# Smaller banks for transposed scores, one more for the rest: PSUM split anew in an attention and expert kernel

## What is computed

```python
sup = relu(sup_feat @ W_fc.T + b_fc)              # 8 x 1601 x 256
ref = relu(layernorm(x) @ W_fc.T + b_fc)          # 8 x 256 x 256
q, k = ref @ W_q.T + b_q, sup @ W_k.T + b_k       # in 16 heads of 16
p = softmax(einsum('bqhd,bkhd->bhqk', q, k) / 4)
out_h = einsum('bhqk,bkf->bhqf', p, sup)
attn = einsum('bhqf,hjf->bqhj', out_h, Wv) + b_v
x = x + ref + attn
x = x + experts(layernorm(x)) + shared(layernorm(x))
```

## Time and profile before

| | |
|---|---|
| median of three runs | 1262.87 us |
| span of the profiled execution | 1261.2 us |
| TensorE busy | 1210.1 us (96%) |
| TensorE weight loads | 910.0 us (72%) |
| VectorE busy | 800.7 us (63%) |
| ScalarE busy | 689.0 us (55%) |
| GpSimd busy | 361.0 us (29%) |
| exponentials (L607), 416 | 412.9 us |
| maxima of side scores (L781), 1024 | 535.2 us |

### The profile page before, as it was taken

One profiled execution on the slowest core, in us unless ns is written; L12 is line 12 of the kernel. 1 busy time (PEld: TensorE's weight loads), 2 busy tenths in 40 slices (PEclk: granted clock), 3 DMA queues, 4 the chain that ended last, 5 costly groups with the idle time before them and its releaser, 6 DMA issues. The chain is left out here.

```text
span 1261.2 us, 23345 instructions
## 1 busy us (share of the span) xinstructions
PE 1210.1 (96%) x8574; PEld 910.0 (72%) x8574; DVE 800.7 (63%) x1682; ACT 689.0 (55%) x954; POOL 361.0 (29%) x282
## 2 busy tenths in 40 slices
PE   7789999999999999999999999999999997999997
PEld 6667777777777777777777777766556885788885
DVE  4566676777777776767777676777855442444443
ACT  4446666666666666666666666656674222222221
POOL 2103233322332232323232233311202651233332
PEclk8999999999999999999999999999999998999999
DMA  5686566678768666677776666666344939733332
GB/s 146 198 229 182 171 184 172 187 208 217 211 200 236 200 191 205 193 209 217 204 220 188 195 185 172 173 187 154 87 132 174 361 129 352 217 55 51 56 53 37
DMA packets 162284, 224.94 MB, mean 178 GB/s; under 512 B 65583, under 2 KB 132023, under 8 KB 162174
## 3 DMA queue, kind: packets, MB, share of 16 engines
q1 hardware_dynamic: 147998, 191.12, 53.2%
q0 software_dynamic: 9216, 16.46, 6.1%
q10 hardware_dynamic: 4960, 15.86, 3.6%
HBM read 128.40 MB, written 93.58 MB: 176 GB/s over the span
## 5 line engine op out<-in xcount | busy, mean ns | idle before, releaser
L781 DVE TENSOR_REDUCE mx<-side 128x1 f32<-128x400 f32 (+2 forms) x1024 | 535.2, 569 | 145.6 <-PE side L505 133.9
L607 ACT ACTIVATE prob<-st 128x1024 f32<-128x1024 f32 (+1 forms) x416 | 412.9, 1022 | 180.2 <-PE st L526 178.4
L505 PE MATMUL side<-kst,qst 96*128 96x400 f32 (+2 forms) x1024 | 325.8, 377 | 4.0 <-DVE mx L781 2.6
L505 PEld LDWEIGHTS side<-kst,qst 96*128 96x128 f32 x1024 | 186.9, 188 | 114.0 <-issue 42.0
L526 PE MATMUL st<-qst,kst 97*128 97x512 f32 (+1 forms) x832 | 264.7, 400 | 1.1 <-ACT prob L607 0.4
L538 PE MATMUL acc<-prob,v 128*32 128x256 f32 (+1 forms) x3328 | 208.1, 383 | 0.0
L526 PEld LDWEIGHTS st<-qst,kst 97*128 97x128 f32 (+1 forms) x832 | 148.1, 186 | 10.4 <-ACT prob L607 2.3
L814 POOL TENSOR_TENSOR clo<-raw,chi 128x768 fp32r<-128x768 f32 (+1 forms) x32 | 60.8, 1902 | 319.5 <-ACT chi L643 319.5
L538 PEld LDWEIGHTS acc<-prob,v 128*32 128x32 f32 (+1 forms) x3328 | 94.2, 109 | 80.2 <-issue 23.6
L1715 POOL DMA_INDIRECT out<-yg,rows_of x39 | 60.8, 1558 | 163.3 <-DMA out<-yg,rows_of 104.3
L820 POOL TENSOR_TENSOR flo<-fc,fhi 128x768 fp32r<-128x768 f32 (+1 forms) x26 | 49.9, 1918 | 180.1 <-ACT fhi L659 180.1
(11 more groups left out here) (197 smaller groups left out, 1687.5 us busy)
## 6 DMA issues: line engine op xcount, KB each, us to landing
kst<-parts_at SPq DMA_DIRECT2D x90, 400.2 KB, 5.8
parts_at<-parts SPq DMA_DIRECT2D x48, 384.0 KB, 6.6
wall<-w_at ACTq DMA_DIRECT2D x10, 1536.0 KB
w_at<-piece_hi SPq DMA_DIRECT2D x27, 512.0 KB, 6.7
w_at<-piece SPq DMA_DIRECT2D x27, 512.0 KB, 5.9
v<-v_at SPq DMA_DIRECT2D x32, 408.0 KB
raw<-ctx_t SPq DMA_DIRECT2D x24, 384.0 KB, 5.5
piece<-gate_up SPq DMA_DIRECT2D x18, 512.0 KB, 4.7
```

The lines of the kernel that those rows point to most:

```text
L505: pe.matmul(side[u.bank][:, 0:w], t.qst[0:96, pair, col * P:(col + 1) * P], t.kst[0:96, pair, o:o + w], start=True, stop=True).then_inc(si ...
L607: act.activation(prob[0:rows, s, :], st[(KT * g + s) % 2][0:rows, :], ACT.Exp, scale=float(DH) ** -0.5).then_inc(exp_done, 1)
L781: dve.tensor_reduce(mx[:, p % 2, hq, r:r + 1], side[u.bank][:, 0:ranges_of(p)[r][1]], AX.X, ALU.max)\
```

## The change

The eight banks are shared out as 4 + 3 + 1. `BANKS` is 4, so a unit waits for the unit four ahead of it. The transposed scores get three tiles `st` of one bank (`SCORE_BANKS`), one for each pair of heads in turn, over all phases (`pair_tile`). Each of the two matmuls of a tile waits for the exponential three pairs earlier and tells ScalarE by itself. The exponential of a key tile goes in two, 128x512 each, and each waits for its own matmul. The product with the values waits for the second of them as before. The functions that counted units in a loop over batches go, since every unit's number is known.

```diff
-BANKS = 3
+BANKS = 4
+SCORE_BANKS = 3
...
+def pair_tile(p, s, i):
+
+    return GP * (KT * p + s) + i
...
-        st = [ctx.enter_context(nc.psum_tensor(f"st{i}", [P, 4 * NQ], F32)) for i in range(2)]
+        st = [ctx.enter_context(nc.psum_tensor(f"st{i}", [P, 2 * NQ], F32)) for i in range(SCORE_BANKS)]
...
-            after(pe, exp_done, KT * p + s - 1)
-            rows, into = key_rows(s), st[(KT * g + s) % 2]
+            rows = key_rows(s)
             for i in range(GP):
-                mm = pe.matmul(into[0:rows, i * 2 * NQ:(i + 1) * 2 * NQ],
-                               t.kst[0:97, GP * g + i, s * P:s * P + rows],
-                               t.qst[0:97, GP * g + i, :], start=True, stop=True)
-            mm.then_inc(st_full, 1)
+                n = pair_tile(p, s, i)
+                after(pe, exp_done, n - SCORE_BANKS + 1)
+                pe.matmul(st[n % SCORE_BANKS][0:rows, :], t.kst[0:97, GP * g + i, s * P:s * P + rows],
+                          t.qst[0:97, GP * g + i, :], start=True, stop=True).then_inc(st_full, 1)
 
         def pe_values(pe, p, b, g, kt):
             rows = key_rows(kt)
-            pe.wait_ge(exp_done, KT * p + kt + 1)
+            pe.wait_ge(exp_done, pair_tile(p, kt, GP - 1) + 1)
...
         def act_exp(act, p, g, s):
             rows = key_rows(s)
-            act.wait_ge(st_full, KT * p + s + 1)
             after(act, pv_done, KT * (p - 1) + s + 1)
...
-            act.activation(prob[0:rows, s, :], st[(KT * g + s) % 2][0:rows, :], ACT.Exp,
-                           scale=float(DH) ** -0.5).then_inc(exp_done, 1)
+            for i in range(GP):
+                n = pair_tile(p, s, i)
+                act.wait_ge(st_full, n + 1)
+                act.activation(prob[0:rows, s, i * 2 * NQ:(i + 1) * 2 * NQ], st[n % SCORE_BANKS][0:rows, :], ACT.Exp,
+                               scale=float(DH) ** -0.5).then_inc(exp_done, 1)
```

More of the change, by code:

```diff
@@ L218, with __init__ @@
 class Unit:
[L222 to L226, removed]
+    def __init__(self, n):
+        self.n, self.bank, self.used = n, n % BANKS, n // BANKS
     def full(self):
-        return self.count(self.n + 1, UNITS)
+        return self.n + 1
     def out(self):
-        return self.count(self.n // BANKS + 1, UNITS // BANKS)
+        return self.used + 1
     def free(self):
-        return self.count(self.n // BANKS, UNITS // BANKS)
+        return self.used
 PRE_AT = {u: n for n, u in enumerate([u for u in PRE if u[0] not in NO_BANK])}
@@ L247 @@
                     AT_END += 1
[L248 to L251, removed]
 def before_unit(u):
@@ L258, in body_unit @@
 def body_unit(b, at, g, kind, arg):
-    n = BODY_AT[at, g, kind, arg]
-    return Unit(n) if isinstance(b, int) else Unit(n, b - at)
+    return Unit(BODY_AT[at, g, kind, arg])
 def ranges_of(p):
@@ L901, in sp_lent_free @@
             unit_full(sp, body_unit(b, b, g, "S1", SCORES - 1))
-            sp.wait_ge(exp_done, KT * (LENT_FROM - 1) + 8)
+            sp.wait_ge(exp_done, pair_tile(LENT_FROM - 1, 8, 0))
             sp.wait_ge(mx_done, LENT_FROM + 1)
@@ L1017, in resid_unit @@
                 return before_unit(("xres", 0, 0))
-            return body_unit(b - 1, at - 1, 1, "xres", 0) if isinstance(b, int) else                 Unit(BODY_AT[1, 1, "xres", 0] - UNITS, b - 1)
+            return body_unit(b - 1, at - 1, 1, "xres", 0)
         def last_scores(units):
```

## The result

The changed kernel takes 1252.59 us (median of six runs, 1249.26 to 1256.68) where the kernel before took 1263.76 us beside it: a ratio of 0.9908, 95% interval 0.989 to 0.9926. That is 11.2 us faster; 1247 us, 15.5 us faster, was forecast. The profiled execution spans 1252.1 us.

A forecast was written before the change was run, and what follows sets the result against it. TensorE, held by late weight loads waiting for banks, was taken to bound the kernel. Side banks -34, start -6.5 and transposed scores +25 gave -15.5 us: from 1262.9 to 1247 us, range 1229 to 1268.

The forecast's parts named there:

- What bounds the kernel: Attention, 180 to 840 us: TensorE sets the pace, and loads waiting for banks lose 27 us in 660.
- Side banks, -34 us in the phases: Side scores and projections: a fourth bank removes the waits for banks, 1.1 us a phase over 31 phases; bounds -17 and -45.
- Ring of three, +25 us: Transposed scores at four short steps wait for the tile before's exponential, 0.8 us a phase over 31 phases; bounds +12 and +40.
- late by x costs x less 0.08: Weight loads on TensorE: a load late by x costs x less some 0.08 us.
- Exponentials: ScalarE: 832 halves at 0.60 us, 0.50 apart in a run, 33 us more ScalarE work; by itself nothing.
- The start, -6.5 us: Before 82 us: at most 3.5 us won before the keys' limit, 2.7 us free behind it; bounds -3 and -12.
- The last phase: Transposed scores of the last phase: counted within the +25 us, at 0.8 us a phase.
- small handshake: Rival: of the transposed scores' short steps only tile 2 to 3 costs, +12; 1228 us; chance 0.18.
- Given back: Rival: half of the side banks' gain returns as VectorE's backlog; 1264 us, no change; chance 0.15.
- Slower: Rival: exponential halves don't overlap, 0.65 us start to start, +26; 1273 us; chance 0.16 shared with the other slower rival.
- The banks give nothing: Rival: the named bank waits are for something else, only added cost remains; 1288 us; chance 0.16 shared with the other slower rival.
- one sign of being wrong: 180 to 840 us: waits for prob over 1.2 us a phase would show the forecast wrong.

The follow-up runs named there:

- The square: Four kernels on one chip: side banks 3 or 4 by single banks 3 or 4, without the nine-bank corner; 1262.56 (kernel before), 1261.46, 1279.77 and 1251.67 us.
- e2: Kernel before with halved exponentials, three side banks, three single banks for the transposed scores, eighth bank unused; 1279.77 us, ratio 1.0127 to the kernel before.
- e5: Changed kernel with the values of tile 1 moved ahead of its first side score, so the vst copy comes sooner; 1250.54 us, ratio 0.9888 to the kernel before.
- e1: Kernel before with halved exponentials, three side banks and four single banks for the transposed scores; 1261.46 us, ratio 0.9993 to the kernel before.
- e4: The changed kernel itself, four side banks and three single banks, run again beside the kernel before; 1251.67 us, ratio 0.9899.
- e12: Changed kernel with side scores and xfc reordered, and two large start transfers issued behind the first row of maxima; 1230.51 us, ratio 0.9725 to the kernel before.

## Why the prediction was right, and where it was off

**What bounds the kernel**: right. TensorE's starts, not its busy time, showed the losses, and the waits named there are the ones that went.

**Side banks, -34 us in the phases**: right, in kind and in size. All that isn't a pair of transposed scores got 32.3 us shorter over thirty phases, 1.08 us each where 1.1 was taken. The square seems to say otherwise: from e2 to the changed kernel the lead grows from 4.8 us at phase 1 to 30.4 at phase 31, 25.6 us. But the 8.3 us of bank waits that the ring's stalls had already swallowed in e2 belong to what was priced. The price of a wait holds there too: by the rule of the prediction the 69 and 51 waits that e2 has left are worth 69 x 0.14 + 51 x 0.17 = 18.3 us in 660, 0.78 us a phase, and 0.85 was gained.

**Ring of three, +25 us**: right in size for the phases. The pairs cost 0.72 us a phase more in the changed kernel and 0.77 in e2, where 0.8 was taken; that e2 falls behind the kernel before by only 14.9 us from phase 1 to 31 (and 2.5 in the last phase, 17.3 in all) is the other side of the same 8.3 us. Place by place it was near. A load that is 0.31 us late at tile 9 costs 0.18 us (0.65 for 0.47 us), as forecast; tile 3 costs 0.36 us, 0.44 was forecast; tile 10 costs 0.14 us, 0.17 was forecast; tile 10 behind xfc costs 0.6 us, and 0.17 with 0.3 added was taken. The second transposed score can't start its load before 1.15 us behind the first one of the tile before; 1.10 was worked out. Two readings were wrong. For tile 3 I named the wrong holder: the copy to vst costs next to nothing there, as e5 shows, and the step alone is too short. And no kind of phase is spared at tile 3: all four lose 0.36 to 0.44 us, while one was counted with 0.4 less. The rule "late by x costs x less 0.08" was a little hard, 0.13 to 0.14 fits these loads.

**Exponentials**: right. 768 of 0.601 us and 64 with 65 rows of 0.593 (0.60 was taken), in runs 0.48 to 0.49 us apart (0.50), and e1 shows no gain and no cost. The group, and a run of four in the timeline:

```profile
L605 ACT ACTIVATE prob<-st 128x512 f32<-128x512 f32 x768 | 406.0, 601 | 147.8 <-PE st L524 144.0
```

```profile
506.68 2.06 ACT L605 ACTIVATE prob<-st 128x512 f32<-128x512 f32 x4
```

The rule of the Trainium skill ("ScalarE: Activation LUTs", What ACT_TABLE_LOAD costs), 186 ns and 0.833 ns an element, gives 612 ns, 11 more than measured, and with its 93 ns of overlap 0.52 us apart in a run; the trace is a little faster on both.

**The start, -6.5 us**: wrong in its size, -3.2 us at phase 0 and -1.9 at phase 1. Up to the row of maxima the forecast held. The sixteen gaps of the earlier trace rows, 11.1 us, are one of 0.40 us. The keys' limit at 63.5 us was right: the score that needs them waits 1.07 us for them and runs at

```profile
62.76 0.67 PE L502 MATMUL side<-kst,qst 96*128 96x450 f32 x2 [1.07 <-DMA kst<-parts]
```

It runs 4.2 us sooner than before, and 2.6 us more are won behind it up to 70 us, where 2.7 were called free. The step that failed is that the sum ends there: it puts the landing of the next DMA, that of the row of maxima, and the clock at nothing. The same data has to move in less time. A DMA of queries (`qst<-q_at`) that held TensorE for 1.12 us before holds it for 2.62 us at 38.75; the row takes 6 us and not 3.3, and holds it for 3.79. After that the lower clock lasts until 84.1 us, and phase 0 takes 1.3 us longer than before.

The clock also blurs what the square says of the start. e2 begins phase 0 2.2 us behind the kernel before and 2.5 behind e1, whose code up to there differs in the number of `st` tiles alone. e2 was granted the lower clock for some 10 us between 43 and 64 us, where e1 wasn't. The stretch from 40 to 50 us, e2 and then e1:

```profile
40.00:50.00 10.00, 7.93 (x30) 6.80 (x30) 4.91 (x10) 3.31 (x6) 1.82 (x1) 0.66 0.63 196
40.00:50.00 10.00, 7.00 (x42) 5.80 (x40) 6.14 (x11) 3.97 (x6) 1.82 (x1) 1.00 0.61 194
```

So the 5.4 us between e2 and the changed kernel at phase 0 aren't the bank's alone. From e1 to the changed kernel it is 3.0 us (81.71 to 78.75); the rest goes most likely with e2's clock.

**The last phase**: about 1 us was forecast within the 25. It costs 2.5 us, 16.0 us from its first to its last transposed score where it was 13.5; this term was too small. Only those and the values stand there, and its matmuls and loads wait 18 times (us, times):

```profile
  ACT prob L605: 8.4, 18
```

So the two large terms, -33 and +24 us for thirty phases, gave -9 where -10.8 was measured, and no luck was needed for them. What is left of the error of 4 us is the start (4.6 us less than forecast), the last phase (it costs 2.5 us, and its shares of the two terms make it -0.3) and the experts (1.0, within the 6 us by which they differ among all these traces), less 1.8 us that the phases gave more and 2 us that the medians fell more than the traces.

**The rivals**: "small handshake" falls by e2 (17 us) and by the trace, where all four places cost. "Given back" falls too: VectorE's waits all but vanish. "Slower" falls: the halves overlap. "The banks give nothing" falls by e2 and e4 (28 us).

**The signs**: one sign of being wrong came true, though the sum held. The waits for prob are 35.3 us in 24 phases, 1.45 us a phase, over the 1.2 named. It was badly set: the idle time of a load isn't its cost, and the late times in the prediction (0.27, 0.26, 0.27 and 0.52 us) already add up to 1.3. Such a wait is some 0.5 us at tile 3, as forecast (0.76 twice), but the one at tile 10 behind xfc is longer, 0.73 us. The other signs are as forecast: two waits of L502 for VectorE, none for fc, and halves 0.49 us apart.

## What to carry to other kernels

A buffer that is read in pieces can be freed in pieces, and a bank of PSUM won so is worth what the waits of its new owner cost. Waits that stand right behind a new stall go with either change, so parts that are measured one by one don't add up. But take a ring's loop time (here 1.15 us from a matmul through ScalarE to the matmul that reuses the bank) and compare it with the shortest steps of the order. Then change order and buffers together: the banks gave 0.9% here, the order alone lost 2.3%, and both together gave 2.3%.

When an engine that was idle comes early, look at the next thing that it will wait for. A small transfer on the way deserves to be issued ahead of large ones that are not urgent yet.

## What the runs showed of the hardware

- A transfer of 4 KB was used 5.5 to 6.1 us after its issue from SP's queue (seven traces) and 6.9 us from ScalarE's (one), while earlier large ones were on their way; with two of these behind it, it took at most 2.6 us, and at most 3.3 us in the kernel before, where they had been issued 8 to 10 us ahead of it.
- A weight load that waits costs about its lateness less 0.13 us, so that 0.3 us late costs 0.18 us of TensorE. Such losses don't show in its busy time.
- ScalarE overlaps the end of one 128x512 exponential with the start of the next by 0.11 us even where each has a semaphore wait of its own.
- Ahead of phase 0 TensorE idled 3.8 us in the changed kernel and was granted the lower clock for about 10 us around it, from 1 us before that wait; in e12, where the longest gap there is 0.9 us, it was about 3.4 us.
- Executions of the same start differed: e2 had some 10 us at the lower clock between 43 and 64 us and e1 none, and it came 2.5 us later to phase 0.
